# Softmax sums of 14 of 16 attention units a layer: rows on TensorE, a contiguous trip through DRAM, and a scaling on GpSimd

## The reference

```python
def attn_block(xq, ctx, Wq, Wk, Wv, Wo, bo, pe_q, pe_k, mask):
    q = (xq @ Wq).reshape(b, n, HEADS, DH).transpose(0, 2, 1, 3)
    ...
    q = q * DH ** (-0.5)
    q = apply_rope(q, pe_q)
    k = apply_rope(k, pe_k)
    sim = jnp.einsum('bhid,bhjd->bhij', q, k)
    if mask is not None:
        sim = jnp.where(mask[:, None, None, :], sim, -jnp.finfo(sim.dtype).max)
    a = jax.nn.softmax(sim, axis=-1)
    out = jnp.einsum('bhij,bhjd->bhid', a, v)
    out = out.transpose(0, 2, 1, 3).reshape(b, n, INNER)
    return out @ Wo + bo
...
for l in range(DEPTH):
    h = rmsnorm(x, sg[l])
    x = attn_block(h, h, sWq[l], sWk[l], sWv[l], sWo[l], sbo[l], pe_q, pe_q, mask) + x
    h = rmsnorm(x, cg[l])
    x = attn_block(h, chunked_seq, cWq[l], cWk[l], cWv[l], cWo[l], cbo[l], pe_q, pe_k, None) + x
    h = rmsnorm(x, fg[l])
    x = jax.nn.gelu(h @ fW1[l] + fb1[l], approximate=False) @ fW2[l] + fb2[l] + x
```

## Time and profile before

| | |
|---|---|
| Median of 3 runs | 1327.59 us (1326.98 to 1330.36) |
| Span of the profiled execution | 1334.7 us |
| TensorE, VectorE, ScalarE, GpSimd busy | 1161.6, 779.1, 706.8, 554.6 us |
| The four layers | about 66 to 976 us of the span |
| Mean granted TensorE clock | 0.947 |

### The profile page before, as it was taken

The page is one execution under the profiler, slowest core; times in us unless marked ns, Lnnn a source line. Parts: engine busy times, 40 slices in busy tenths (PEclk is TensorE's granted clock), DMA queues, the critical chain, the costliest instruction groups (busy, mean ns, idle before and its releaser), DMA issues.

```text
span 1334.7 us, 21229 instructions
## 1 busy us (share of the span) xinstructions
PE 1161.6 (87%) x7374; PEld 766.2 (57%) x7374; DVE 779.1 (58%) x2164; ACT 706.8 (53%) x1889; POOL 554.6 (42%) x643
## 2 busy tenths in 40 slices
PE   4399998979999897999988899988669976897898
PEld 2255564655556566565556555555559964454687
DVE  7766655476665557666555766565352235775455
ACT  2177665547766536767543776655144433563332
POOL 2467543467754347766236677433221010111110
PEclk8699999999999999999999999999879988998899
DMA  4001010001111000200100020100111100000010
GB/s 139 16 10 17 17 40 9 25 1 39 25 17 41 25 1 1 47 17 17 41 25 1 1 49 17 33 1 1 48 52 33 49 0 1 1 1 1 9 36 26
DMA packets 60857, 31.00 MB, mean 23 GB/s; under 512 B 34260, under 2 KB 52049, under 8 KB 60753
## 3 DMA queue, kind: packets, MB, share of 16 engines
q1 hardware_dynamic: 60753, 29.64, 8.6%
HBM read 28.47 MB, written 1.16 MB: 22 GB/s over the span
## 4 chain that ended last, share of the span: by engine, by line
PE 69%; DVE 13%; POOL 6%; DMA 6%; ACT 4%; issue 2%; SPq 0%; POOLq 0%; DVEq 0%
PE bank L1644 11%; PE bank L1598 7%; PE bank L1704 7%; PE bank L1621 7%; PE bank L1861 4%; DMA dram_r<-recs 4%; PE bank L2081 3%; PE bank L1672 3%; PE bank L1792 3%; PE bank L1794 2%; PE bank L1793 2%; PE bank L1655 2%; PE bank L1590 2%; DMA recT<-dram_r 2%; PE bank L1675 1%
## 5 line engine op out<-in xcount | busy, mean ns | idle before, releaser
L937 DVE CUSTOM_DVE_ANT_0 bank<-bank,maskrow 128x512 f32<-128x512 f32 x256 | 172.1, 715 | 96.2 <-PE bank L1598 95.0
L1343 ACT ACTIVATE probs<-bank,tops 128x512 f32<-128x512 f32 x256 | 174.3, 685 | 99.0 <-DVE tops L937 98.3
L1355 ACT ACTIVATE KA<-bank 128x512 f32<-128x512 f32 x256 | 139.0, 600 | 25.2 <-PE bank L1621 20.5
L1598 PE MATMUL bank<-QR 64*128 64x512 f32 x768 | 126.1, 436 | 16.7 <-DVE rot L926 12.1
L1621 PEld LDWEIGHTS bank<-ident,probs 128*128 128x128 f32 x1024 | 117.0, 141 | 38.6 <-issue 26.3
L1644 PE MATMUL bank<-KA,Vs 128*64 128x512 f32 x512 | 135.4, 615 | 3.9 <-DVE AT L960 3.9
L1621 PE MATMUL bank<-ident,probs 128*128 128x128 f32 x1024 | 134.3, 274 | 2.3 <-ACT Vs L1315 2.3
L1339 ACT ACTIVATE probs<-bank,tops 128x154 f32<-128x154 f32 x256 | 96.5, 387 | 67.9 <-DVE tops L934 66.8
L925 DVE TENSOR_TENSOR rot<-bank,cos 128x512 f32<-128x512 f32 (+1 forms) x112 | 73.5, 656 | 63.8 <-PE bank L1675 54.6
L1598 PEld LDWEIGHTS bank<-QR 64*128 64x128 f32 x768 | 65.2, 189 | 44.2 <-issue 24.2
L703 POOL TENSOR_TENSOR rot<-rot,sin 128x512 f32<-128x512 f32 x48 | 61.2, 1276 | 61.9 <-DVE rot L926 61.9
(11 more groups left out here) (274 smaller groups left out, 2545.8 us busy)
## 6 DMA issues: line engine op xcount, KB each, us to landing
recT<-dram_r SPq DMA_DIRECT2D x56, 128.0 KB, 3.3
W<-in_W SPq DMA_DIRECT2D x8, 256.0 KB, 3.1
Vc<-in_wup SPq DMA_DIRECT2D x8, 192.0 KB, 2.4
W<-in_sWk SPq DMA_DIRECT2D x4, 256.0 KB, 4.2
W<-in_sWq SPq DMA_DIRECT2D x4, 256.0 KB, 4.4
W<-in_sWv SPq DMA_DIRECT2D x4, 256.0 KB, 4.7
wo<-in_sWo SPq DMA_DIRECT2D x4, 256.0 KB, 3.8
ck<-in_cWk SPq DMA_DIRECT2D x4, 256.0 KB, 2.8
```

What stands on the lines that cost most here:

```text
L937: v.tensor_tensor_reduce(bank[i][:, :], bank[i][:, :], maskrow[:, u.b * S:(u.b + 1) * S], -SCALE, 3.0e38, ALU.add, ALU.min, tops[:, g % 4, ...
L1343: c.activation(to, bank[i][:, :], ACT.Exp, bias=tops[:, g % 4, e, 0:1], scale=-1.0, accum_out=sums[:, n, e, k:k + 1]).then_inc(q.probs_rea ...
L1355: c.activation(turned_self(u)[:, half, :, k * P:(k + 1) * P], bank[4 + half][:, :].rearrange("p (c t) -> p c t", t=P), ACT.Copy).then_inc( ...
L1598: ins = mm(bank[first + e][:, :], QH[rows_of(e), u.j, a, w], KH[rows_of(e), u.j, c, :], start=(n == 0), stop=(n == 2))
```

## The change

NEAR shrinks from nine units to two (7 and 15), so 14 units of a layer go through DRAM. For these, TensorE turns the 128 x 8 sums into 8 rows of 128 in bank 5, in the last step of the unit (`turn_sums`); VectorE takes the reciprocal of these rows straight out of bank 5 into `recrow`; SP writes `recrow` to DRAM as 8 contiguous rows and reads it back as before. VectorE copies bank 6 to AT unscaled as soon as it is full, and GpSimd multiplies AT by `recT` later, at steps that SCALED lists (`scale_heads`). The two slots of `recT` are now counted by rows sent and have a semaphore each. `sout` and `cout` wait for `heads_scaled` too. For units 7 and 15 ScalarE copies bank 7 into AT itself, and VectorE multiplies it there. To make room, `triu` lies in `cos` and is made on GpSimd after the layers instead of at the start, and `gates` lies in `ctxK`.

```diff
-NEAR = tuple(range(7, 16))
+SCALED = {u: 4 * u + 6 for u in range(8)}
+
+SCALED.update({8 + c: min(36 + 2 * c, 47) for c in range(7)})
+
+NEAR = (7, 15)
...
+def slot(n):
+
+    return rows_sent(n) % 2
...
+                    scale=[units[i] for i, t in SCALED.items() if t == s and i not in NEAR],
...
+        recrow = sb("recrow", [2 * TB, 2, P])
...
-        triu = sb("triu", [P, P])
         cos = sb("cos", [P, S]); sin = sb("sin", [P, S])
+        triu = cos[:, 0:P]
...
-        gates = sb("gates", [P, TILES, E])
+        gates = ctxK[:, 0:TILES * E].rearrange("p (t e) -> p t e", e=E)
...
 
                 i = u.n % 4
                 sp.wait_ge(q.rec_ready, u.n + 1)
-                sp.dma_start(dram_r[i].rearrange("e t p -> p (e t)"), recs[:, i, :, :].rearrange("p e t -> p (e t)"),
-                             allow_slow_non_contiguous=True).then_inc(q.rec_out, 16)
+                sp.dma_start(dram_r[i].rearrange("e t p -> (e t) p"), recrow[:, rows_sent(u.n) % 2, :]).then_inc(q.rec_out, 16)
                 sp.wait_ge(q.rec_out, 16 * rows_sent(u.n))
-                if u.n >= 2:
-                    sp.wait_ge(q.heads_ready, u.n - 1)
+                if rows_sent(u.n) > 2:
+                    sp.wait_ge(q.heads_scaled, rows_sent(u.n) - 2)
                 for e in range(2):
-                    sp.dma_start(recT[e * DH:e * DH + DH, u.n % 2, :],
-                                 dram_r[i, e].rearrange("t p -> (t p)").partition_broadcast(DH)).then_inc(q.spread_in, 16)
+                    sp.dma_start(recT[e * DH:e * DH + DH, slot(u.n), :],
+                                 dram_r[i, e].rearrange("t p -> (t p)").partition_broadcast(DH)).then_inc(
+                                     (q.spread_in0, q.spread_in1)[slot(u.n)], 16)
...
+            def scale_heads(u):
+
+                pool.wait_ge(q.heads_ready, u.n + 1)
+                pool.wait_ge((q.spread_in0, q.spread_in1)[slot(u.n)], 32 * ((rows_sent(u.n) + 1) // 2))
+                o = AT[:, u.j, u.b * S:(u.b + 1) * S]
+                g.tensor_tensor(o, o, recT[:, slot(u.n), :], ALU.mult).then_inc(q.heads_scaled, 1)
...
+                    for u in step.scale:
+                        scale_heads(u)
...
+            g.memset(triu, 1.0).then_inc(q.pool_step, 1)
+            pool.wait_ge(q.pool_step, see.next(q.pool_step))
+            g.affine_select(out=triu, in_=triu, compare_op=ALU.is_ge, fill=0.0, base=0,
+                            pattern=[[1, P]], channel_multiplier=-1).then_inc(q.triu_ready, 1)
...
             def reciprocals(step):
 
-                dve.wait_ge(q.probs_ready, 2 * step.g + 2)
                 n = step.unit.n
-                v.reciprocal(recs[:, n % 4, :, :], sums[:, n % 4, :, :]).then_inc(q.rec_ready, 1)
+                if n % (2 * UNITS) in NEAR:
+                    dve.wait_ge(q.probs_ready, 2 * step.g + 2)
+                    v.reciprocal(recs[:, n % 4, :, :], sums[:, n % 4, :, :]).then_inc(q.rec_ready, 1)
+                else:
+                    dve.wait_ge(q.sums_full, rows_sent(n))
+                    if rows_sent(n) > 2:
+                        dve.wait_ge(q.rec_out, 16 * (rows_sent(n) - 2))
+                    v.reciprocal(recrow[:, rows_sent(n) % 2, :], bank[5][0:2 * TB, 0:P]).then_inc(q.rec_ready, 1)
 
             def normalise(u):
 
+                o = AT[:, u.j, u.b * S:(u.b + 1) * S]
                 if u.n % (2 * UNITS) in NEAR:
                     dve.wait_ge(q.spread_ready, u.n + 1 - rows_sent(u.n))
+                    dve.wait_ge(q.weighed, u.n + 1)
+                    v.tensor_tensor(o, bank[6][:, :], o, ALU.mult).then_inc(q.heads_ready, 1)
                 else:
-                    dve.wait_ge(q.spread_in, 32 * rows_sent(u.n))
-                dve.wait_ge(q.weighed, u.n + 1)
-                v.tensor_tensor(AT[:, u.j, u.b * S:(u.b + 1) * S], bank[6][:, :], recT[:, u.n % 2, :],
-                                ALU.mult).then_inc(q.heads_ready, 1)
+                    dve.wait_ge(q.weighed, u.n + 1)
+                    v.tensor_copy(o, bank[6][:, :]).then_inc(q.heads_ready, 1)
...
             def spread_out(u):
                 act.wait_ge(q.spread_full, u.n + 1 - rows_sent(u.n))
-                c.activation(recT[:, u.n % 2, :], bank[7][:, :], ACT.Copy).then_inc(q.spread_ready, 1)
+                c.activation(AT[:, u.j, u.b * S:(u.b + 1) * S], bank[7][:, :], ACT.Copy).then_inc(q.spread_ready, 1)
...
+            def turn_sums(u):
+
+                free(5)
+                turn(bank[5][0:2 * TB, 0:P], sums[:, u.n % 4, :, :].rearrange("p e t -> p (e t)"),
+                     ident[:, :]).then_inc(q.sums_full, 1)
+                reader[5], read_at[5] = q.rec_ready, u.n + 1
...
                 elif p.what in ("sout", "cout"):
                     cross = p.what == "cout"
                     pe.wait_ge(q.w_cout if cross else q.w_sout, 16 * (p.l + 1))
-                    pe.wait_ge(q.heads_ready, ((p.l * 2 + cross) * B + b + 1) * PAIRS)
+                    last = ((p.l * 2 + cross) * B + b + 1) * PAIRS
+                    pe.wait_ge(q.heads_ready, last)
+                    pe.wait_ge(q.heads_scaled, rows_sent(last - 1))
...
+                    if step.unit and step.k == step.unit.tiles - 1 and step.unit.n % (2 * UNITS) not in NEAR:
+                        turn_sums(step.unit)
```

More of the change, by code:

```diff
@@ L32 @@
 SCALE = DH ** -0.5
-CONSTS = 3
+CONSTS = 2
 NEG = -float(2.0 ** 100)
@@ L80 @@
 DONE = {u: at[-1] for u, at in WEIGH.items()}
-NEAR = tuple(range(7, 16))
+SCALED = {u: 4 * u + 6 for u in range(8)}
+SCALED.update({8 + c: min(36 + 2 * c, 47) for c in range(7)})
+NEAR = (7, 15)
 def rows_sent(n):
     return sum(i % (2 * UNITS) not in NEAR for i in range(n + 1))
+def slot(n):
+    return rows_sent(n) % 2
 Unit = namedtuple("Unit", "n l cross b j tiles end")
-Step = namedtuple("Step", "unit k g before after weigh spread done pieces dve late")
+Step = namedtuple("Step", "unit k g before after weigh spread done scale pieces dve late")
 Piece = namedtuple("Piece", "what l b j unit step bank early")
@@ L111, in __init__ @@
                 u = Unit(2 * UNITS * l + i, l, cross, b, j, tiles, first + tiles - 1)
-                bare += [Step(u, k, first + k, None, None, (), (), (), (), True, False) for k in range(tiles)]
+                bare += [Step(u, k, first + k, None, None, (), (), (), (), (), True, False) for k in range(tiles)]
         self.steps.append(self.alone(BEFORE, -1, None, bare[0:2]))
@@ L131, in alone @@
     def alone(self, text, l, last, first):
-        return Step(None, 0, None, None, None, (), (), (), self.pieces(text, l, last and last.unit, last, first), False, False)
+        return Step(None, 0, None, None, None, (), (), (), (), self.pieces(text, l, last and last.unit, last, first), False, False)
     def pieces(self, text, l, unit, last, first):
@@ L423, in decoder @@
             turned_dve = sem("turned_dve")
+            sums_full = sem("sums_full")
             spread_full = sem("spread_full")
@@ L426, in decoder @@
             rec_out = sem("rec_out")
-            spread_in = sem("spread_in")
+            spread_in0 = sem("spread_in0")
+            spread_in1 = sem("spread_in1")
+            heads_scaled = sem("heads_scaled")
             mv_ready = sem("mv_ready")
@@ L472, in decoder @@
             xpad_zero = sem("xpad_zero")
+            triu_ready = sem("triu_ready")
             xs_full = sem("xs_full")
@@ L643, in _ @@
             g.memset(ident[:, :], 0.0)
-            g.memset(triu[:, :], 1.0)
             g.memset(ones64[:, :], 1.0)
@@ L653, in _ @@
                             pattern=[[0, 1]], channel_multiplier=1).then_inc(q.const, 1)
-            g.affine_select(out=triu[:, :], in_=triu[:, :], compare_op=ALU.is_ge, fill=0.0, base=0,
-                            pattern=[[1, P]], channel_multiplier=-1).then_inc(q.const, 1)
             pool.wait_ge(q.pool_step, see.next(q.pool_step))
@@ L1129, in decayed @@
                 link(v.memset(ones_row, 1.0))
+                dve.wait_ge(q.triu_ready, 1)
                 for b in range(B):
@@ L1150, in decayed @@
                             v.tensor_copy(SC[:, i, (i + 1) * P:], src[:, (i + 1) * P:])
-                        v.tensor_tensor(SC[:, i, i * P:(i + 1) * P], src[:, i * P:(i + 1) * P], triu[:, :],
+                        v.tensor_tensor(SC[:, i, i * P:(i + 1) * P], src[:, i * P:(i + 1) * P], triu,
                                         ALU.mult).then_inc(q.sc_ready, 1)
```

## The result

The changed kernel takes 1337.43 us (median of 6 executions, 1330.66 to 1338.92), the kernel before 1328.97 (6 executions, 1325.41 to 1333.47): ratio 1.0058, 95% interval [1.0033, 1.0082]. It is slower by 8.5 us where 9.7 us less were forecast. The profiled execution took 1338.92 us, with a span of 1337.2 us and a mean granted clock of 0.933.

A forecast was written before the change was run, and what follows sets the result against it. TensorE, busy 87%, was taken to bound the self half, while it often waits in the cross half. Terms -5 - 12 + 3.7 + 3.6 = -9.7 us gave 1318 us from a 1327.59 median; forecast 1311 to 1324, range 1303 to 1337.

The forecast's parts named there:

- The walk through the cross half: Second layer's cross half, step by step: of 9.2 us gross from removed spreads and bank waits, 2.4 us arrives.
- 3.2 for each of the other three: Cross halves of the other three layers: 3.2 us gain each, because a half-clock stretch falls on step 40.
- 1.66 us behind VectorE: Cross half, after steps 34 and 44: without the spread the next step waits 1.66 us for VectorE instead of 0.69.
- about 1.2 us of `cout0` for the scaling: Cross half, step 43: TensorE waits about 1.2 us because unit 11's scaling stands behind other GpSimd work.
- 0 for units 1 to 6: Self half: the wait for the longer reciprocal holding bank 5 is hidden, costing 0; bounds 0 or 0.35 us a unit.
- Unit 0's 0.9 us: Self half, unit 0: ScalarE empties bank 5 late, costing 0.9 us a layer, 3.6 us in all.
- The 3.7 us for transposes: Self half: 28 added transposes of sums at 0.13 us each, all on the path, cost 3.7 us.
- The DMA wait: Normalise: the copy to AT no longer waits for DRAM, worth 3.9 to 6.4 us; 5 taken.
- the third, bank 5: Self units wait 0.35 us or more on bank 5, transposes cost 0.27 us: 1338 us, slower; 20% chance.
- The second: Cross half: GpSimd's scalings delay packed tails and ropes by 1.28 us each, taking back the gain: 1324 to 1333 us; 20%.
- The first: Self half: TensorE's busy time hides slack, so transposes and waits cost nothing: 1310.6 us, or 1293 if ropes keep up; 18%.
- The sign against the forecast: Self half: the forecast is wrong if TensorE waits on the reciprocal in every self unit; no size given.

The follow-up runs named there:

- before_again: The kernel before, run again unchanged to see the granted clock of each execution: 1330.33 us, mean clock 0.943 to 0.949 in its 10 executions.
- before_fill: The kernel before plus useless TensorE matmuls at five places where TensorE waits: 1327.18 us, ratio 0.9984 to the kernel before.
- before_fill_less: The kernel before plus useless TensorE matmuls, their number fitted to the waits: 1320.11 us, ratio 0.9945 to the kernel before.
- the experiment without turned sums: Against the kernel before, units 0 to 6 only: unscaled copy, scaling on GpSimd, but scattered write and no transposed sums; 1325.89 us, ratio 0.9972.
- the mixed version: Against the kernel before: units 0 to 6 scaled on GpSimd without transposed sums, units 8 to 14 as in the change, no useless matmuls; 1329.92 us, 1.0013.
- dead_spread: The whole change with the 28 removed spreads put back as dead work into bank 7: 1339.68 us, ratio 1.0081 to the kernel before.

## Why the prediction was wrong

- **The step that failed first**: the clock has no term in the sum. The walk through the cross half took a half-clock stretch of the kernel before as 0.8 us more gain in three layers, and never asked what becomes of the clock when 0.97 us of matmuls goes seven times a layer from a half in which TensorE already waits. It falls, for 14.6 us in the change against 7.3 before. The walk itself held: 2.4 us forecast for the second layer, 2.7 - 0.6 = 2.1 measured at full clock. But its 3.2 for each of the other three rested on half-clock stretches of one execution, so that 12 us stood where 10.8 - 1.8 = 9.0 came. Its waits held too: 1.66 us behind VectorE (1.57), about 1.2 us of `cout0` for the scaling (1.45).
- **The second**: "0 for units 1 to 6", the wait for the reciprocal "hidden, with 0.1 us to spare". The duration was right (0.95 forecast, 0.942 measured). The 0.1 us came from the transpose pushing the next matmuls back by 0.13 us; it pushes them by 0.03. And the load of the second four doesn't run ahead: it starts 0.12 us after the reciprocal's end. That is 0.23 us in step 7 and 0.22 to 0.24 at most units, inside the bounds of 0 to 0.35, but 0.40 in step 24; with 0.1 behind unit 0 it is 1.6 us a layer: 6.4 us where 0 stood. Unit 0's 0.9 us came in as 0.85. The 3.7 us for transposes came in as what is left, some 0.6. Together 10.4 us where 7.3 stood.
- **The DMA wait**: 5 us forecast from the one trace, and that execution holds 4.9 us of it: step 8 takes 5.0 and 4.7 us instead of 3.7 in two layers, step 32 takes 6.3, 6.8 and 6.9 instead of 5.8 in three. But it was a long one, its span 7.1 us over the median, and the traces of before_again, before_fill and before_fill_less hold only 0.8, 0.6 and 0. So the term was right for its execution and too large for the median from which it was taken. By the experiment without turned sums it is at most 3.7 [2.0, 5.3], and it goes without them.
- **The size of the miss**: from 9.7 us less to 8.5 us more is 18.2 us. The clock is some 7 to 8 of it, the DMA wait up to 5, the self half 3.1, the cross half 3.0.
- **The rivals**: the third, bank 5, named 1338 us, nearly the time, by luck: its 14 us for waits and transposes came in as some 7, and the clock, which it doesn't name, makes up the rest. The wait reached the 0.4 us from which it was to decide in step 24 alone. The second named the right place at `cout0`, once a layer, not three times. The first fell: weight loads are busy 65.6 of 115.8 us in the self half, and still each 0.2 us of wait there lengthened it. The Trainium skill (Perfetto Trace Analysis, "Identifying the Most-Contended Engine") would judge TensorE's headroom by its weight loads; here that would have misled.
- **Signs named ahead**: reciprocals of 0.95 us and copies without DMA came true; so did "without waits on VectorE's reciprocal" by the profile's brackets, which name ScalarE there. It took an experiment to see that they were wrong. The sign against the forecast, a wait on the reciprocal in every self unit, had come true. So the self windows grew by 2.6 us a layer, not by one or two.

The Trainium skill (TensorE: Matmul & The Clock Gate, "What's actually happening") puts the penalty of the ramp to full clock, over a kernel's first matmuls, at less than 1% of a typical span. What the runs here show is another loss: the full clock is lost again within the layers, and by the ratios this costs the change 1.10%, with TensorE busy 87% of the span.

## What to carry to other kernels

Before you take work off an engine whose clock follows its load, look at the granted clock of the stretch, and ask whether the work sat in waits: there it costs little and may hold the clock for all around it. Compare two kernels at the same clock (fill the waits of both) before you judge an edit of 1%. Who holds a PSUM bank counts by the time until it lets go: empty it with a short copy and do the slow operation elsewhere.

## What the runs showed of the hardware

- Useless matmuls in TensorE's waits made the kernel before 0.55% faster ([0.36, 0.75]%), the mixed version 19.7 us faster. In the cross half of the change low stretches came behind waits of 1.3 to 1.9 us, in that of the kernel before behind waits of 1.65 and 1.71 us; but none came behind the 1.89 us ahead of `cq1.0` in the four layers of dead_spread, so the length of one wait does not tell.
- A reciprocal of 8 x 128 out of PSUM takes 942 ns, a copy of the same 275 ns. The 1.07 us that was worked out as an estimate by the rule in the Trainium skill (VectorE: DVE Perf Modes, "First, the fixed hardware budget") is 0.13 us too long; the line through two rows was closer.
- One transpose of 128 x 8 sums between other matmuls moves the next by 0.03 us, not by the 0.13 us that a transpose takes in a row of its like the earlier trace rows.
